# A mixture-of-experts kernel on one core: where the second layer's expert outputs are written, and by which queue

## What is computed

```python
weights_BSK, indices_BSK = jax.lax.top_k(probs_BSE, TOP_K)          # TOP_K = 2
norm_weights_BSK = jax.nn.softmax(weights_BSK, axis=-1)
...
gating_BSEF = jnp.einsum('BSD,EDF->BSEF', x, kernel_gating_EDF)      # D = 128, F = 256, E = 8
act_BSEF = jax.nn.silu(gating_BSEF)
up_BSEF = jnp.einsum('BSD,EDF->BSEF', x, kernel_up_EDF)
down_BSED = jnp.einsum('BSEF,EFD->BSED', act_BSEF * up_BSEF, kernel_down_EFD)
out_BSD = jnp.einsum('BSED,BSE->BSD', down_BSED, full_weights_BSE)
```

## Time and profile before

| | us |
|---|---|
| median of three executions | 678.43 |
| the three | 678.43, 678.68, 673.98 |
| span of the profiled execution, first to last instruction | 673.9 |
| PE busy | 519.5 (77%) |
| DVE busy | 453.6 (67%) |
| ScalarE busy | 206.2 (31%) |
| POOL busy | 181.0 (27%) |

### The profile page before, as it was taken

One profiled execution on the slowest core, in us unless ns is written; L12 is line 12 of the kernel. 1 busy time (PEld: TensorE's weight loads), 2 busy tenths in 40 slices (PEclk: granted clock), 3 DMA queues, 4 the chain that ended last, 5 costly groups with the idle time before them and its releaser, 6 DMA issues.

```text
span 673.9 us, 17842 instructions
## 1 busy us (share of the span) xinstructions
PE 519.5 (77%) x7491; PEld 356.3 (53%) x7491; DVE 453.6 (67%) x927; ACT 206.2 (31%) x369; POOL 181.0 (27%) x147
## 2 busy tenths in 40 slices
PE   5537789888988898875599948775987889797752
PEld 4325566665766666643344433235876757643522
DVE  6897678777878696857577828951444436838845
ACT  2212434443454345331224410021222223413221
POOL 4271221222040304057317833000000001046631
PEclk9765799999999999997879969895799999998765
DMA  8555113232513243001002250430465655411211
GB/s 227 156 152 164 55 55 115 72 95 62 155 56 105 61 121 115 9 13 44 16 5 64 60 133 18 112 98 15 132 182 172 186 174 155 136 37 38 62 36 31
DMA packets 79183, 62.26 MB, mean 92 GB/s; under 512 B 10080, under 2 KB 72320, under 8 KB 79104
## 3 DMA queue, kind: packets, MB, share of 16 engines
q1 hardware_dynamic: 69408, 51.39, 26.5%
q0 software_dynamic: 3072, 6.30, 3.2%
q10 hardware_dynamic: 6624, 3.44, 1.8%
HBM read 44.10 MB, written 12.32 MB: 84 GB/s over the span
## 4 chain that ended last, share of the span: by engine, by line
PE 46%; DVE 18%; issue 11%; SPq 5%; ACT 4%; DMA 3%; POOL 2%; another core or an unknown queue 0%; DVEq 0%; ACTq 0%; POOLq 0%
PE ps L898 6%; PE ps L846 5%; PE ps L1013 4%; DVE small L1207 3%; DMA BIG<-in_wd 3%; SPq L638 3%; DVE small L1170 3%; DVE BIG L1175 3%; PE ps L854 2%; PE ps L914 2%; PE ps L885 2%; PE ps L744 2%; PE ps L797 2%; PE ps L932 2%; PE ps L1021 2%
## 5 line engine op out<-in xcount | busy, mean ns | idle before, releaser
L1798 POOL TENSOR_TENSOR BIG<-BIG,small 128x2048 f32<-128x2048 f32 x14 | 51.5, 3685 | 190.2 <-DVE small L1183 190.2
L1780 POOL DMA_INDIRECT xs<-BIG,small x48 | 54.5, 1135 | 38.3 <-DVE small L1098 24.3
L1835 POOL TENSOR_TENSOR BIG<-BIG 128x512 f32<-128x512 f32 x4 | 4.8, 1210 | 161.8 <-DVE BIG L1501 161.8
L1013 PE MATMUL ps<-BIG 128*128 128x128 f32 x312 | 44.9, 289 | 3.0 <-DVE BIG L1144 1.9
L846 PEld LDWEIGHTS ps<-BIG 128*128 128x128 f32 x368 | 44.7, 192 | 3.4
L846 PE MATMUL ps<-BIG 128*128 128x128 f32 x368 | 44.7, 275 | 0.0
L898 PE MATMUL ps<-XT,BIG 128*128 128x512 f32 x96 | 44.1, 618 | 0.0
L1170 DVE TENSOR_REDUCE small<-ps 128x64 f32<-128x1024 f32 x32 | 39.0, 1218 | 7.2 <-PE ps L744 7.2
L1787 POOL DMA_INDIRECT BIG<-ys,small x32 | 31.8, 994 | 41.3 <-PE ps L885 26.9
L1013 PEld LDWEIGHTS ps<-BIG 128*128 128x128 f32 x312 | 40.4, 202 | 4.2 <-ACT BIG L1583 3.1
L1207 DVE TENSOR_REDUCE small<-ps 128x8 f32<-128x1024 f32 x32 | 37.7, 1217 | 7.0 <-PE ps L775 5.5
(11 more groups left out here) (253 smaller groups left out, 1094.9 us busy)
## 6 DMA issues: line engine op xcount, KB each, us to landing
BIG<-in_w SPq DMA_DIRECT2D x23, 512.0 KB, 3.7
BIG<-in_w SPq DMA_DIRECT2D x23, 256.0 KB, 3.8
BIG<-in_wg SPq DMA_DIRECT2D x39, 128.0 KB, 2.2
BIG<-in_wu SPq DMA_DIRECT2D x39, 128.0 KB, 2.3
BIG<-in_wd SPq DMA_DIRECT2D x39, 128.0 KB, 2.5
BIG<-BIG SPq DMA_DIRECT2D x64, 71.4 KB
ys<-BIG SPq DMA_DIRECT2D x62, 64.0 KB, 2.1
xs<-BIG SPq DMA_DIRECT2D x14, 256.0 KB, 3.2
```

What stands on the lines that cost most here:

```text
L1013: t = e.matmul(bank(s)[:, i:i + 128], WT[(NTL[0] + j) % NWT][:, i:i + 128], XsT[(NTL[0] + j) % 2], start=True, stop=True)
L1780: e.indirect_dma_start(XSd[L], bass.IndirectOffsetOnAxis(ap=posi[:, 16 * k + n:16 * k + n + 1], axis=0), xn[:, n, :], None).then_inc(d_sca ...
L1798: e.tensor_tensor(v, v, bc_last(zz[i], 16), ALU.mult).then_inc(p_ready, 1)
```

## The change

A row in the sorted table of the second layer, now called `rows1`, is 144 values wide instead of 128. Value 128 holds, as an integer, the row's own place in a second DRAM table `home1`, which is in token order: 16k + tile number, times 128, plus the partition, for choice k; rows that no token takes name places behind the 4096 real ones. POOL makes these numbers (`iota` into `ids`) and writes them into `XN1` before the scatters (`name_rows`), once for choice 0 and then, after the first choice's scatters of the same tiles have landed, for choice 1. The empty rows, with their numbers, are made in SBUF as `blank` (39 x 144 values a partition) by POOL early in the program, and `clear(1)` writes them with three DMAs instead of ten.

`y1` is no longer a step of SP. POOL writes each of the 39 tiles to `home1` with one indirect DMA, whose places are the tile's own value 128; for this the tiles' rows are fetched into a ring `XR` of ten, which are kept until their tile is written. At the end SP waits until all are written and loads `home1` back with four plain loads of 512 KB each (even and odd tiles, each choice) into `YA`, which lies where the weights `WT` were. `back` on DVE reads `YA`. The 32 gathers and their waits are gone.

```diff
-            def store(L, j):
-                J = j + NTL[0] * L
-                w.wait_ge(psum.empty(("y1" if L else "y0", j)))
-                e.dma_start(YSd[L][128 * j:128 * j + 128, :], YS[J % 3]).then_inc(d_ys[J % 3], 16)
+            def store(j):
+                w.wait_ge(psum.empty(("y0", j)))
+                e.dma_start(YSd[0][128 * j:128 * j + 128, :], YS[j % 3]).then_inc(d_ys[j % 3], 16)
...
                 elif s[0] == "x1":
                     fetch(1, s[1])
-                elif s[0] == "y1":
-                    store(1, s[1])
+            rows = YSd[1][0:2 * T, :].rearrange("(k n p) d -> p k n d", k=2, p=128)
+            w.wait_all(ys_stored(1))
+            for u in range(2):
+                for k in range(2):
+                    e.dma_start(YA[:, k, u:NT:2, :], rows[:, k, u:NT:2, :]).then_inc(d_ya[u][k], 16)
...
             def sorted_out(s, J, cols):
                 w.wait_ge(psum.full(s))
                 if J >= 3:
-                    w.wait_ge(d_ys[J % 3], 16 * (J // 3))
+                    w.wait_ge(row_stored(J - 3))
...
-            def back(idx, n, weight):
-                w.wait_ge(d_ga[idx % 4], 16 * (idx // 4 + 1))
+            def back(idx, n, k, weight):
+                w.wait_ge(d_ya[n % 2][k], 16)
...
-                    w.wait_ge(psum.full(("h0", J - 4) if J - 4 < NTL[0] else ("h1", J - 4 - NTL[0])))
-                    e.dma_start(XS[J % 4], XSd[1][128 * j:128 * j + 128, :]).then_inc(d_xs[J % 4], 16)
+                    if j >= NXR:
+                        w.wait_ge(psum.full(("h1", j - NXR)))
+                        w.wait_ge(row_stored(J - NXR))
+                    e.dma_start(XR[j % NXR], XSd[1][128 * j:128 * j + 128, :]).then_inc(d_xr[j % NXR], 16)
...
+            e.memset(blank, 0.0).then_inc(blank_ready, 1)
+            e.iota(ids, [[128, 71]], base=0, channel_multiplier=1).then_inc(blank_ready, 1)
...
                 if k == "scatter1":
+                    kk, n = s[1] // NT, s[1] % NT
                     w.wait_ge(pos_ready, 2)
                     w.wait_ge(d_zero[1], ZERO_ALL[1])
-                    scatter(1, s[1] // NT, s[1] % NT, XN1)
+                    if kk and n % 8 == 0:
+                        w.wait_ge(d_first[n // 8], 16 * 8)
+                        name_rows(1, n, n + 8)
+                    w.wait_ge(ids_ready, 2 + kk * (n // 8 + 1))
+                    scatter(1, kk, n, XN1, d_scat[1] if kk else d_first[n // 8])
...
-                elif k == "back1":
-                    n, kk = (list(range(0, NT, 2)) + list(range(1, NT, 2)))[s[1] // 2], s[1] % 2
-                    made = [x for x in TWO[:TWO.index(s)] if x[0] == "ro"]
-                    if made:
-                        w.wait_ge(psum.full(("ro",) + made[-1][1:]))
-                    gather(1, s[1], kk, n)
+                elif k == "y1":
+                    j = s[1]
+                    J = NTL[0] + j
+                    w.wait_ge(psum.empty(s))
+                    e.indirect_dma_start(YSd[1], bass.IndirectOffsetOnAxis(ap=XR[j % NXR][:, 128:129].bitcast(I32), axis=0),
+                                         YS[J % 3], None).then_inc(d_home[J % 3], 16)
```

More of the change, by code:

```diff
@@ L18 @@
 NWT = 4
+ROW = 144
+NXR = 10
 ISQ8 = 1.0 / float(np.sqrt(np.float32(8.0)))
@@ L359, in build @@
         YS = [take(128) for _ in range(3)]
-        WT = [take(1024) for _ in range(NWT)]
+        WTf = take(1024 * NWT)
+        WT = [WTf[:, 1024 * k:1024 * k + 1024] for k in range(NWT)]
+        YA = WTf.rearrange("p (k n d) -> p k n d", k=2, n=NT)
         ZR = take(512)
-        GA = [ZR[:, 128 * k:128 * k + 128] for k in range(4)]
+        ids = take(71).bitcast(I32)
         shared = cursor[0]
         W2T = [take(512) for _ in range(4)]
-        take(6144)
+        blank = take(NTL[1] * ROW).rearrange("p (n d) -> p n d", n=NTL[1])
+        take(6144 - NTL[1] * ROW)
         wqT, wkv, wkN, woT = take(128), take(256), take(128), take(128)
@@ L412, in build @@
         S2, U2 = (take(256).rearrange("p (b k) -> p b k", b=8) for _ in range(2))
+        XR = [take(ROW) for _ in range(NXR)]
         LG = take(1024).rearrange("p (i g n) -> p i g n", i=4, g=8)
@@ L506, in build @@
         d_ys = [sem(f"d_ys{k}") for k in range(3)]
-        d_ga = [sem(f"d_ga{k}") for k in range(4)]
+        d_ya = [[sem(f"d_ya{u}{k}") for k in range(2)] for u in range(2)]
         d_back = [sem(f"d_back{b}") for b in range(NB)]
@@ L510, in build, with row_stored, ys_stored @@
         d_stack = [sem(f"d_stack{k}") for k in range(2)]
-        def ys_stored(n):
-            return [(d_ys[k], 16 * ((n - k + 2) // 3)) for k in range(3)]
+        d_home = [sem(f"d_home{k}") for k in range(3)]
+        def row_stored(J):
+            k, j = J % 3, J - NTL[0]
+            return (d_ys[k], 16 * (J // 3 + 1)) if j < 0 else (d_home[k], 16 * (j // 3 + 1))
+        def ys_stored(L):
+            return [row_stored(NTL[0] + NTL[1] * L - 1 - k) for k in range(3)]
+        blank_ready, ids_ready = sem("blank_ready"), sem("ids_ready")
         pool_made, pb_ready = sem("pool_made"), sem("pb_ready")
@@ L549, in clear @@
                 rows = XSd[L].rearrange("(n p) d -> p n d", p=128)
[L550 to L553, removed]
+                if L == 0:
+                    w.wait_ge(pool_made, ZERO)
+                    for n in range(0, NTL[L], 4):
+                        k = min(4, NTL[L] - n)
+                        e.dma_start(rows[:, n:n + k, :], ZR[:, 0:128 * k].rearrange("p (n d) -> p n d", n=k)).then_inc(d_zero[L], 16)
+                else:
+                    w.wait_ge(blank_ready, 3)
+                    for n in range(0, NTL[L], 13):
+                        e.dma_start(rows[:, n:n + 13, :], blank[:, n:n + 13, :]).then_inc(d_zero[L], 16)
             e.dma_start(wqT, io["wqT"]).then_inc(d_w0, 16)
@@ L628, in _ @@
                 elif s[0] == "y0":
-                    store(0, s[1])
+                    store(s[1])
             for s in late(TWO, LATE["SP2"]):
@@ L1802, in _ @@
                     w.wait_ge(d_zero[0], ZERO_ALL[0])
-                    scatter(0, 0, s[1], XN0)
+                    scatter(0, 0, s[1], XN0, d_scat[0])
                 elif k == "mom":
@@ L1814, in _ @@
             e.memset(VP[:, :, 0:31], 0.0).then_inc(pad_ready, 1)
+            e.memset(XN1[:, :, 128:ROW], 0.0).then_inc(ids_ready, 1)
+            w.wait_ge(ids_ready, 1)
+            name_rows(0, 0, NT)
             for s in TWO:
```

55 lines of the change are left out of this document (30 added, 25 removed).

## The result

| | before | after |
|---|---|---|
| median of the timed runs, us | 678.04 (4 runs, 673.98 to 678.68) | 667.10 (4 runs, 663.45 to 668.57) |
| ratio, with its 95% interval | | 0.985 [0.980, 0.989] |
| profiled execution: its span, us | 673.9 | 664.5 |
| its own time, us | not given (in every later run 1.7 to 1.9 over the span) | 666.34 |

Two later sets on other chips gave the change 0.988 [0.978, 0.997] and 0.986 [0.970, 1.001].

What follows compares the result with a forecast made beforehand. SP's queue was taken to bound the tiles to about 545 us, then nearly full PE, then DVE, PE and ScalarE in turn; -9 - 1.7 - 1.0 + 0.7 + 0.5 = -10.5, so 678.4 - 10.5 = 668 us, range 659 to 679.

Steps and rivals of the forecast that it cites:

- SP without the store: Expert tiles: without the store's 0.52 us a tile SP's queue runs faster; gain taken at 9 us, between 0 and 11.1.
- SP's hold-ups as the new limit: Expert tiles: hold-ups of 0.41 us on a bare 2.04 would leave SP the limit, at 2.45 us a tile.
- the second rival: PE sets the pace throughout, hold-ups vanish and weights are never late: -17 us, so 661; chance 0.18.
- The gathers: Tail: DVE's wait for a gather goes (1.7 us) and the second gates speed up (1.0, range 0 to 2.2).
- the loads: Tail: four loads replace 32 gathers; the additions wait 0 to 2 us for them, taken at 0.5.
- The first gates behind a write: First gates: POOL's first multiplication stands behind tile 30's write, 2.4 us late; cost 0 to 1.3 us, taken at 0.7.
- POOL's writes: Expert tiles: 39 indirect writes at 1.27 us each, gap included, keep under the tile's 2.45 us; taken at 0.
- The rival that they become the limit: Expert tiles: most POOL writes take 2915 ns, its period is 3.2 us, and the kernel takes 686 us; chance 0.15.
- Start and scatters: Start and both layers' scatters: clearing `blank`, larger clears and wider rows are covered by existing waits; cost nothing.
- the cover: Second layer's scatters: POOL's wait of 14.2 us covers 8 us of small copies and longer scatters.
- PE's waits for `in_wd` at 2 to 3 us: Sign in the expert tiles: PE's waits for the down weights, 11.1 us before, would be 2 or 3 us.
- SP's period at 2.45: Sign in the expert tiles: SP's period between gating fetches would be about 2.45 us in place of 2.97.

Runs made afterwards that it cites:

- the relief alone: The kernel before with the second layer's 39 stores issued by POOL as plain stores, all else as it was: 654.69 us against 662.41, ratio 0.990 (chip 9).
- the small store: The changed kernel with an 8 KB store (16 rows) per tile put back on SP: 675.01 us against 664.50, ratio to before 1.005 (chip 11).
- the two relieved kernels: On chip 9, the kernel before with its 39 stores issued by POOL (654.69 us), and the changed kernel with POOL's writes three steps later (644.88 us).
- the same edit: The kernel before with its 32 gathers replaced by four plain loads of the sorted table: 658.84 us against 662.41, ratio 0.996 (chip 9).
- the idle gathers: The changed kernel with 32 gathers put back on POOL into a ring that nobody reads: 676.06 us against 664.50, ratio to before 1.006 (chip 11).
- the third profile of before: The kernel before, unchanged, profiled a third time, on chip 8; median there 674.62 us.
- the third of after: The changed kernel, unchanged, profiled a third time, on chip 8: 663.89 us, ratio to before 0.986.
- the later writes: The changed kernel with POOL's 39 writes three steps later: 644.88 us, ratio to before 0.977 (chip 9); 664.79 us against 663.89 for the changed kernel (chip 8).

## Why the prediction was right, and where it was wrong

The sum was right, -10.5 forecast and -10.9 measured. The mechanism was right in the tiles, where SP's queue set the pace, and in the tail only in part. The terms were not right; several errors cancelled, so that the sum came out so close is luck. By the mean of two profiles of before and three of after on the chips where PE pauses:

**SP without the store, forecast -9: stage C gave -6.2.** That SP's queue sets the pace is shown twice, by the relief alone (-8.4) and by the small store (+6.8 in stage C). The step that failed was the value for SP's hold-ups as the new limit, a period of 2.45 us. They stayed (1.04 and 1.12 us in place of 0.38 for single issues) but did no harm, since SP now waits for PE: PE sets the pace, as the second rival said for this stretch, at 2.03 us where it runs freely. It then meets a limit of its own, which no step of mine had. From the first to the last of the steady tiles the profiles show 55.9 and 56.1 us before and 50.5 and 50.6 after, with 3.1 and 2.9 us of pauses at the small matmuls (line 906); on chip 9, without them, the two relieved kernels took 47.2 and 46.9 against 57.0. So where PE didn't pause the stage gave 8.4 to 8.7 us, and the forecast of 9 was good.

**The gathers, forecast -2.7, and the loads, +0.5: stage E gave -8.5.** On chip 9 it was -2.8 for the same edit, and the loads cost nothing in any profile. The rest is PE's pauses beside the gathers, a term that the prediction didn't have: 8.4 to 9.4 us before, none after, and the idle gathers brought 8.0 us of them back. The row was before me, the 1.98 us of the earlier trace rows, which is put down to "issue" and not to DVE. I read it as an echo of DVE's wait; it was the other thing. Not all of it reaches the end: when the additions are over earlier, DVE waits for PE's large matmuls instead. The last section of the tail, from the additions beside the last transposes on, grew by 1.9 us (18.6 to 20.5 by the means), in a wait that was 1.35 us in the third profile of before and is in the third of after

```profile
643.76 0.72 DVE L1059 STREAM_TRANSPOSE BIG<-ps 128x512 f32<-128x512 f32 x1 [3.73 <-PE ps L1015]
```

**The first gates behind a write, forecast +0.7, bounds 0 to 1.3.** Up to the end of the first gates' chain stage D grew from 37.9 to 39.1 us, +1.2, and the later writes took 1.5 off again on one chip (38.7 to 37.2). I had the order right, and missed that the late multiplications now meet the next of DVE's operations with two SBUF inputs: the pair takes 0.68 + 2.87 us where it took 1.57 + 0.69 before, 1.3 us more, and 2.87 is the very price that I let go from the second gates. The row of 2.87 agrees with the Trainium skill's "SBUF — State Buffer" on the shared port pair, where such an operation and a GpSimd operation that reads SBUF exclude each other: 0.69 us alone, 2.87 beside the two of 1.07. By the same page I had allowed 0.5 us more for the writes; they took 957 ns, so that allowance wasn't needed. Over the whole of stage D 0.8 us is lost.

**POOL's writes, forecast 0: right.** 957 ns at the median, 1153 at most, DVE never waits. The rival that they become the limit, from 2.67 us on, is out.

**Start and scatters, forecast 0: not settled.** Stage A is 341.5 to 347.6 us in the five profiles that have before's first layer, mean 345.2, and 342.5 to 349.3 in the seven that have after's, mean 346.4. The chips are not spread evenly over the two: without chip 9 two profiles have the first of these layers, mean 342.5, and six the second, mean 347.1; on chip 9 it is three, mean 346.9, and one, 342.5. So the profiles fit a loss of several microseconds here as well as none. Stage B moved by +0.9, within its spread of 2.5 on these chips. For the second layer's scatters the cover held: POOL still waits 13.1 us behind them, where it was 14.2. (The larger clears write 12.5% more bytes, 144 values for 128, and not 15%; nothing hangs on it.)

**The signs that I named.** PE's waits for `in_wd` at 2 to 3 us: they vanished. SP's period at 2.45: PE's 2.03 took its place, see above. The last copy at about 582 us: it came at 592.6, since stages A and B were 5.5 us longer in that profile, the tiles gave less, and the gates cost more. A first addition 10 to 11 us after the last copy: 8.5 us.

The terms at their measured values, -6.2 + 0.8 - 8.5 + 0.9 (stage B), are -13.0. In the same five profiles stage A grew by 6.2 (342.5 to 348.7), which leaves -6.8, while the medians of the three sets differ by -10.9, -8.3 and -10.7. By them stage A lost some 2 to 5 us, an estimate from these differences; why it should, no run shows. I also took the runs' 4.5 us above the profiled span as fixed; after the change it was 2.6 (667.10 less 664.5), chance of the same kind.

## What to carry to other kernels

Where a queue of DMA issues sets the pace of a loop, what counts is the number of its issues and what they wait for, and not their bytes: 39 stores of 8 KB cost as much as 39 of 64 KB. Before a gain is put down to the engine that was freed, read what the next engine does at its own limit, with its small instructions. And take a second profile of an unchanged kernel before stages of two kernels are compared; here two of them differed by 13 us in places that nobody had touched.

## What the runs showed of the hardware

In the first set and on chips 8 and 11 PE pauses at runs of small matmuls (32x32 and 32x64) while POOL has indirect DMAs under way. It starts a few of them and then waits 0.3 to 2.3 us with no cause that the profile shows: 8.5 to 9.2 us in stage B beside the scatters, 2 to 3 in the tiles beside the writes, 8.0 to 9.4 in the tail beside the gathers. On chip 9 the same three places had at most 1.2 us of it. In the tail the pauses left with the gathers and came back with unread ones, so there the indirect DMAs are shown to be the condition; in the tiles line 906's pauses came with the writes; for stage B it is argued, since nothing was taken away there. Why it happens stays open. The fetches of PE's instructions (16 KB each) took 0.9 to 1.9 us in all these stretches, on either kind of chip, and stood at other times than most of the pauses, so their length doesn't explain it.

Not every pause put down to "issue" is of this kind. At the head of stage C, with POOL idle, every one of the fourteen profiles, chip 9's too, has five pauses in front of runs of about 60 + 60 small matmuls (L951 and L941 of before), together 8.1 to 10.4 us. The first two of the first profile of before, then of the second (chip 9):

```profile
454.15 0.98 PE L951 MATMUL ps<-BIG 32*32 32x16 f32 x59 [2.21 <-issue]
457.49 0.98 PE L951 MATMUL ps<-BIG 32*32 32x16 f32 x58 [1.43 <-issue]
```

```profile
448.39 0.99 PE L951 MATMUL ps<-BIG 32*32 32x16 f32 x59 [2.00 <-issue]
452.00 0.98 PE L951 MATMUL ps<-BIG 32*32 32x16 f32 x58 [1.70 <-issue]
```

Each has its own fetch of 16 KB of instructions: in the first profile of before they start at 451.69, 455.29, 458.59, 462.49 and 466.34 us, take 0.9 to 1.5 us, and PE goes on 1.2 to 1.4 us after each has ended. In all fourteen profiles that last distance is 1.2 to 1.5 us. So these pauses go with the instruction fetches, one to one; that they are caused by them no run tests. The same distance, 1.2 to 1.5 us, holds for the one or two pauses of 0.6 to 2.3 us that line 932 has behind the last scatters in all profiles but one.

Single issues on SP now and then took 0.9 to 2.2 us in place of 0.38 in every kernel, with the store or without it.
